# Turning the context rows on VectorE instead of TensorE in the attention stage

## The chip, the cores and the metric

The kernel runs on one core of a Trainium2 chip. The metric is the device time of one execution in microseconds. TensorE multiplies matrices (its results go to PSUM banks), VectorE and ScalarE move and compute between SBUF and PSUM, GpSimd computes on SBUF, and SyncE issues the DMAs. Each engine works through its own queue in order; semaphores connect them.

## What is computed

A layer with cross attention and a feed-forward network, in fp32:

```
x:   [16, 112, 1024]      ctx: [16, 375, 1024]
q = layernorm(x) @ Wq     (32 heads of 32)
k = ctx @ Wk,  v = ctx @ Wv   (8 KV heads of 32, each used by 4 query heads)
x = x + softmax(q k^T / sqrt(32)) v @ Wo
h = silu(y @ w1^T) * (y @ w3^T),  y = layernorm(x)      (inner width 3584)
x = x + h @ w2^T          (weights are w * w_scale per 128x128 block)
```

The products need the 1024 context columns on the partitions, so every context (375 rows of 1024) has to be transposed before K and V can be computed. That transposition is what changes.

## The kernel before

The program has a query stage, the attention stage, an output stage ("mixing") and the feed-forward stage. Every fp32 product is made of three: each operand is split into a high part (rounded to the fp32r type, on ScalarE) and a low part (the rest, `to_lo` on VectorE, line 90), and lines 84 to 86 add high x high, high x low and low x high in PSUM.

The attention stage is written as a pipeline of bodies (`each`). Body b does four things at once for four batches: attention proper for batch b (`attn`), the row maxima of the scores of batch b+1 (`score`), the K and V projections of batch b+2 (`proj`), and the transposition of context b+3 (`trans`). Bodies run from -3 to 15. Body -3 only transposes; bodies -2 and -1 have no attention proper; bodies 0 to 12 do all four; body 13 has no context to transpose; 14 and 15 run out. Each body has 32 steps, and each engine's queue is the list of its work step by step. The tables give the steps:

```
T_STEP = {3: 0, 9: 1, 15: 2, 21: 3, 26: 4, 30: 5}     # step: tile of the context
KV_TILES = 3*[[2,1,1,1,1,2]] + [[2,2,1,1,2],[2,2,2,1,1]]   # K0 K1 V0 V1 V2, from step 1
INV = {25, 27, 28, 31: batch b; 5, 8, 11, 14: batch b-1}    # reciprocals of the sums
```

Per step TensorE scores one head of batch b+1 against all keys (two heads at steps 18 and 24, none at 30 and 31) into one of two banks; VectorE takes the maximum over the keys (L696), and head h is scored only once head h-2 has its maximum. Then come one or two of the eight accumulation steps of a K or V tile, and at steps 6 to 29 a score matmul in the other direction (L907), whose exponential ScalarE takes (L800). At steps 19 and 31 TensorE multiplies the exponentials by V ("PV", L924), at steps 2 and 22 it adds their sums over the partitions (L816). GpSimd first adds the exponentials of three key blocks, per group of 16 heads in two adds of 125x1792: the first (L649) when eight exponentials are there, so after steps 13 and 25, the second (L645) when twelve are; and it scales the result (L656). All these operands of GpSimd are in SBUF. A body ends and begins with the transpose of the maxima at step 0 (L842), whose bank VectorE splits (L688 and L90) for the next steps.

A context tile n before the change is a block of 125 rows by 512 columns (four 128-column pieces). TensorE transposes the four pieces against a unit matrix into one PSUM bank (L861), ScalarE writes the high part `cT_h` from the bank (L774), VectorE the low part `cT_l` (bank minus high), all listed at the tile's step. TensorE begins K of the next batch (step 1 of the next body) when all six tiles have their low part (`t_lo`). The two banks (`pj_bank`) are shared by the transposes, the K and V tiles and the transpose of the maxima; so several waits of TensorE are about banks. Contexts lie row by row in `stash` (two slots of three blocks) and are loaded by three DMAs of 125 rows with 4 KB each, one body ahead.

## Time and profile before

| | |
|---|---|
| median of 3 runs | 2532.99 us (2530.29 to 2537.29) |
| profiled execution | 2538.41 us, span of the profile 2536.6 us |
| TensorE busy, share of the span | 2427.8 us, 96% |
| VectorE | 1698.4 us, 67% |
| ScalarE | 979.2 us, 39% |
| GpSimd | 559.2 us, 22% |
| transposes of the context (L861) | 384 matmuls, first at 191.4, last at 751.7 |
| maxima (L696) | 512, 264.9 us busy |
| attention stage | some 191 to 850 us of the span |

All times below are microseconds from the start of the span, of one profiled execution. A duration in a row is that of one instruction (or the merged run of several, with xcount). Neighbouring instructions of one engine overlap a little, so the price of one more in a full queue is the distance from its start to the next start. Of a matmul the duration contains the way through the array; its price is again the distance between starts. In square brackets behind a row stands how long the engine was idle before it and what ended that.

### The profile page before, as it was taken

How to read it: one execution, taken by the hardware profiler on the slowest of the kernel's cores; microseconds unless marked ns; L12 is line 12 of the kernel's file. 1: busy time of each engine (PE TensorE's matmuls, PEld its weight loads, DVE VectorE, ACT ScalarE, POOL GpSimd, SP SyncE). 2: the span in 40 equal slices, each digit the busy share in tenths (PEclk: the TensorE clock that was granted, in tenths of full speed). 3: DMA queues.
4: the chain of work that ended last, by engine and by line, in shares of the span. 5: the costliest groups of instructions: out<-in, count | busy, mean ns of one | idle time of the engine just before them, and what ended most of it. 6: DMA issues, size and time to landing. Idle time of an engine off the chain costs nothing.

```text
span 2536.6 us, 35412 instructions
## 1 busy us (share of the span) xinstructions
PE 2427.8 (96%) x12682; PEld 2071.4 (82%) x12682; DVE 1698.4 (67%) x2639; ACT 979.2 (39%) x1673; POOL 559.2 (22%) x305
## 2 busy tenths in 40 slices
PE   7998999999999799599999998999999999999999
PEld 6997878878875488489999987988988978888887
DVE  6425777777776344688888888888888874445442
ACT  3212445445444321354444444444433443233231
POOL 1000344454455300001111111322333320000000
PEclk9998999999998799799999999999999999999999
DMA  7535555555545335456555564565776687555652
GB/s 226 173 92 138 140 139 139 144 134 142 143 110 131 95 127 170 119 183 184 159 176 156 158 179 134 158 174 190 208 209 176 172 287 234 172 174 160 183 161 86
DMA packets 369146, 408.04 MB, mean 161 GB/s; under 512 B 125824, under 2 KB 324096, under 8 KB 359152
## 3 DMA queue, kind: packets, MB, share of 16 engines
q1 hardware_dynamic: 369008, 406.22, 56.1%
q8 instruction: 85, 1.39, 0.2%
q14 instruction: 53, 0.43, 0.1%
HBM read 252.99 MB, written 152.70 MB: 160 GB/s over the span
## 4 chain that ended last, share of the span: by engine, by line
PE 44%; DVE 8%; DMA 3%; issue 2%; SPq 1%; ACT 1%; DVEq 0%; ACTq 0%
PE bank L84 15%; PE bank L85 14%; PE bank L86 14%; DMA stash<-weight_scratch 3%; DVE g_WL L90 2%; DVE g_XL L90 1%; DVE g_su L1699 1%; DVE xT L1655 1%; SPq L1431 1%; DVE stash L1667 1%; DVE stash L1666 1%; DVE stash L1669 1%; ACT stash L1548 0%; ACT g_WH L1558 0%; DVE stash L1643 0%
## 5 line engine op out<-in xcount | busy, mean ns | idle before, releaser
L84 PE MATMUL bank<-g_XH,g_WH 128*128 128x448 f32 (+1 forms) x2254 | 848.0, 376 | 51.8 <-DVE g_su L1699 24.2
L85 PE MATMUL bank<-g_XL,g_WH 128*128 128x448 f32 (+1 forms) x2254 | 845.0, 375 | 0.0
L86 PE MATMUL bank<-g_XH,g_WL 128*128 128x448 f32 (+1 forms) x2254 | 844.8, 375 | 0.0
L84 PEld LDWEIGHTS bank<-g_XH,g_WH 128*128 128x128 f32 x2254 | 425.2, 189 | 115.8 <-DVE g_WL L90 52.8
L86 PEld LDWEIGHTS bank<-g_XH,g_WL 128*128 128x128 f32 x2254 | 425.2, 189 | 54.1
L85 PEld LDWEIGHTS bank<-g_XL,g_WH 128*128 128x128 f32 x2254 | 425.4, 189 | 53.5
L1558 ACT ACTIVATE g_WH<-stash 128x512 fp32r<-128x512 f32 x392 | 241.7, 627 | 427.6 <-PE bank L86 247.0
L90 DVE TENSOR_TENSOR g_WL<-stash,g_WH 128x512 fp32r<-128x512 f32 (+1 forms) x417 | 336.0, 809 | 77.4 <-ACT g_WH L1558 49.4
L696 DVE TENSOR_REDUCE a_nm<-bank 112x1 f32<-112x375 f32 x512 | 264.9, 531 | 116.9 <-PE bank L831 113.3
L800 ACT ACTIVATE a_pr<-bank 125x448 f32<-125x448 f32 x384 | 204.8, 545 | 208.2 <-PE bank L907 153.7
L649 POOL TENSOR_TENSOR a_prsum<-a_pr 125x1792 f32<-125x1792 f32 x32 | 129.3, 4039 | 365.3 <-ACT a_pr L800 365.3
L1699 DVE TENSOR_TENSOR g_su<-bank,g_su 128x448 f32<-128x448 f32 x280 | 170.8, 610 | 35.6 <-PE bank L86 35.3
L831 PE MATMUL bank<-a_kst,a_qst 96*112 96x376 f32 x512 | 183.2, 367 | 5.8 <-DVE a_nm L696 2.6
L907 PE MATMUL bank<-a_qst,a_kst 98*125 98x448 f32 x384 | 148.3, 391 | 2.8 <-ACT a_pr L800 2.4
L831 PEld LDWEIGHTS bank<-a_kst,a_qst 96*112 96x112 f32 x512 | 91.7, 179 | 69.7 <-DVE a_nm L696 32.6
L1498 POOL TENSOR_TENSOR g_Sh<-stash 128x448 f32<-128x448 f32 x28 | 32.6, 1165 | 492.5 <-DVE stash L1704 492.5
L645 POOL TENSOR_TENSOR a_prsum<-a_prsum,a_pr 125x1792 f32<-125x1792 f32 x32 | 128.7, 4022 | 1.8
L678 DVE RECIPROCAL a_l<-a_l 128x112 f32<-128x112 f32 x128 | 106.6, 839 | 25.8 <-ACT a_l L754 25.8
L84 PE MATMUL bank<-a_w_h,a_cT_h 128*125 128x256 f32 x384 | 111.8, 291 | 0.0
L86 PE MATMUL bank<-a_w_h,a_cT_l 128*125 128x256 f32 x384 | 107.8, 281 | 0.0
L85 PE MATMUL bank<-a_w_l,a_cT_h 128*125 128x256 f32 x384 | 107.7, 280 | 0.0
L1285 ACT ACTIVATE g_WH<-stash 128x1792 fp32r<-128x1792 f32 x25 | 42.6, 1703 | 156.8 <-PE bank L86 146.3
(132 smaller groups left out, 3592.8 us busy)
## 6 DMA issues: line engine op xcount, KB each, us to landing
stash<-in_L_ffn_w SPq DMA_DIRECT2D x168, 256.0 KB, 5.1
weight_scratch<-stash SPq DMA_DIRECT2D x28, 1024.0 KB, 7.7
stash<-weight_scratch SPq DMA_DIRECT2D x28, 1024.0 KB, 7.4
h_scratch<-g_Sh SPq DMA_DIRECT2D x112, 224.0 KB, 3.9
down_scratch<-xT SPq DMA_DIRECT2D x98, 256.0 KB, 3.1
stash<-in_ctx SPq DMA_DIRECT2D x48, 500.0 KB
stash<-h_scratch SPq DMA_DIRECT2D x25, 896.0 KB, 6.7
a_qst<-q_scratch SPq DMA_DIRECT2D x96, 224.0 KB, 4.7
```

What stands on the lines that cost most here:

```text
L84: pe.matmul(acc, lh, rh, start=first, stop=False, skip_group_check=onto)
L85: pe.matmul(acc, lh, rl, start=False, stop=False, skip_group_check=onto)
L86: return pe.matmul(acc, ll, rh, start=False, stop=last, skip_group_check=onto)
L90: return nc.vector.tensor_tensor(dst, src, hi.bitcast(f32), ALU.subtract)
L645: pool.tensor_tensor(prsum[:], prsum[:], pr[0:CK, :, 2, :], ALU.add).then_inc(all_added, 1)
L649: pool.tensor_tensor(prsum[:], pr[0:CK, :, 0, :], pr[0:CK, :, 1, :], ALU.add).then_inc(two_added, 1)
L696: nc.vector.tensor_reduce(nm[:, 1 - par, h:h + 1], s_bank[h % 2][0:SQ, 0:SK], AX.X, ALU.max, negate=True).then_inc(max_done, 1)
L800: nc.scalar.activation(pr[0:CK, r, c, :], st_bank[u % 2][0:CK, 0:J * SQ], ACT.Exp, scale=SCALE).then_inc(exp_done, 1)
L831: pe.matmul(s_bank[h % 2][0:SQ, 0:SKP], qst[0:96, 1 - par, g, j * SQ:(j + 1) * SQ], kst[0:96, 1 - par, g, :], start=True, stop=True).then_ ...
L907: pe.matmul(st_bank[u % 2][0:CK, 0:J * SQ], kst[0:98, par, g * R + r, c * CK:(c + 1) * CK], qst[0:98, par, g * R + r, :], start=True, stop ...
L1558: nc.scalar.activation(WH[:, i, :, :], w_source(mi, i), ACT.Copy).then_inc(w_hi, 1)
L1699: nc.vector.tensor_tensor(su[:, slot, :], acc[mi % 2][:, 0:TB], su[:, other, :], ALU.add).then_inc(summed, 1)
```

## The change

The context is loaded in another layout, turned on VectorE, and the split reads SBUF. A batch's context is loaded as four column quarters of 256 columns, one on each 32 partitions, with the rows in blocks of 32: eight DMAs with rows of 1 KB. VectorE's transpose turns 32x32 blocks, so a block transpose of 128 partitions by 512 elements (two row blocks) yields tile n: 64 context rows, all 1024 columns, with column q*256 + 32k + j on partition 32q + j of slice k. The K and V weights are loaded with their rows in that same order. The tile is written to a double buffer `ctT` in a part of `stash` that was free.

The transpose stands at the tile's step on VectorE, behind the maxima and the K or V copy of that step. ScalarE makes the high part at the same step, now from `ctT`. VectorE's low part moves one step later (`s - 1 in T_STEP`). TensorE loses the transposes, and its waits for banks are written anew. The Wo load waits for `t_lo` and `t_hi` as well.

```diff
         def load_ctx(sp, n, slot):
-            for c in range(NC):
-                sp.dma_start(ctx_in[:, slot, c, :], ctx[bass.ds(n, 1), c * CK:(c + 1) * CK, :]
-                             .rearrange("b k n -> k (b n)")).then_inc(c_loaded[slot], 16)
+            for q in range(Q4):
+                cols = slice(q * DQ, (q + 1) * DQ)
+                sp.dma_start(ctx_in[q * BL:(q + 1) * BL, slot, 0:CB - 1, :],
+                             ctx[bass.ds(n, 1), 0:CROWS, cols].rearrange("b (c i) n -> i (b c) n", i=BL)
+                             ).then_inc(c_loaded[slot], 16)
+                sp.dma_start(ctx_in[q * BL:q * BL + SK - CROWS, slot, CB - 1, :],
+                             ctx[bass.ds(n, 1), CROWS:SK, cols].rearrange("b k n -> k (b n)")
+                             ).then_inc(c_loaded[slot], 16)
...
                         for n, w in enumerate((wk, wv)):
-                            sp.dma_start(wkv_raw[:, :, n * KV:(n + 1) * KV],
-                                         w.rearrange("(k p) n -> p k n", p=P)
-                                         ).then_inc(wkv_loaded, 16)
+                            for q in range(Q4):
+                                sp.dma_start(wkv_raw[q * BL:(q + 1) * BL, :, n * KV:(n + 1) * KV],
+                                             w[q * DQ:(q + 1) * DQ, :].rearrange(
+                                                 "(k j) n -> j k n", j=BL)).then_inc(wkv_loaded, 16)
...
-                    c, kh = n // 2, n % 2
-                    return cT[:, 1 - par, 4 * kh:4 * kh + 4, c * CK:(c + 1) * CK]
+                    return cT[:, 1 - par, :, 2 * BL * n:min(2 * BL * (n + 1), SK)]
+
+                ctT = stash[:, 2 * NC + 1, :].rearrange("p (e k n) -> p e k n", e=2, k=KT)
+
+                def turned(n):
+                    return ctT[:, n % 2, :, 0:min(2 * BL, SK - 2 * BL * n)]
...
                                 sp.wait_ge(t_done, NT * B)
+                                sp.wait_ge(t_lo, NT * B)
+                                sp.wait_ge(t_hi, NT * B)
                                 sp.wait_ge(v_moved, B)
                                 load_wo(sp)
...
                                 if trans and s in T_STEP:
                                     n = T_STEP[s]
+                                    if n == 0:
+                                        dve.wait_ge(c_loaded[1 - par], 16 * 2 * Q4 * (i + 2 + par))
+                                    wait(dve, t_hi, NT * tb + n - 1)
+                                    wait(dve, t_lo, NT * tb + n - 1)
+                                    nc.vector.transpose(
+                                        ctT[:, n % 2, :, :].rearrange("p b (c j) -> p b c j", j=BL),
+                                        ctx_in[:, 1 - par, 2 * n:2 * n + 2, :].rearrange(
+                                            "p c (b j) -> p b c j", j=BL)).then_inc(t_done, 1)
+                                if trans and s - 1 in T_STEP:
+                                    n = T_STEP[s - 1]
                                     dve.wait_ge(t_hi, NT * tb + n + 1)
-                                    to_lo(cT_part(cT_l, par, n), t_bank(par, n)[:, 0:4 * CK].rearrange(
-                                        "p (k n) -> p k n", k=4), cT_part(cT_h, par, n)
-                                        ).then_inc(t_lo, 1)
+                                    to_lo(cT_part(cT_l, par, n), turned(n), cT_part(cT_h, par, n)
+                                          ).then_inc(t_lo, 1)
...
                                     nc.scalar.activation(cT_part(cT_h, par, n),
-                                                         t_bank(par, n)[:, 0:4 * CK].rearrange(
-                                                             "p (k n) -> p k n", k=4), ACT.Copy
+                                                         turned(n), ACT.Copy
                                                          ).then_inc(t_hi, 1)
...
-                                if trans and s in T_STEP:
...
-                                    if n == NT - 1:
-                                        pe.wait_ge(t_lo, NT * tb + n)
-                                    elif n == 0 and attn:
-                                        pe.wait_ge(nm_lo, b + 1)
-                                    elif proj:
-                                        accumulated(pe, pb, n - 1)
-                                    else:
-                                        wait(pe, t_lo, n - 1)
-                                    for k in range(4):
-                                        kk = 4 * kh + k
-                                        last = pe.transpose(t_bank(par, n)[:, k * CK:(k + 1) * CK],
-                                                            ctx_in[:, 1 - par, c, kk * P:(kk + 1) * P],
-                                                            ident[0:CK, 0:CK])
-                                    last.then_inc(t_done, 1)
...
                                         pe.wait_ge(t_lo, NT * (pb + 1))
+                                        wait(pe, v_out, NC * pb)
                                     elif ks[0] == 0:
-                                        if trans:
-                                            pe.wait_ge(t_lo, NT * tb + m)
-                                        elif m == 1:
-                                            pe.wait_ge(nm_lo, b + 1)
+                                        if m == 1:
+                                            if attn:
+                                                pe.wait_ge(nm_lo, b + 1)
                                         else:
                                             accumulated(pe, pb, m - 2)
```

On VectorE the end of a body, from step 25 to step 31, stands so before. Here `a_nm` are the maxima, `a_l` the sums to be inverted, `a_cT_l` the low part of a context tile, and the COPY moves a V tile:

```order
L696 TENSOR_REDUCE a_nm<-bank 112x1
L678 RECIPROCAL a_l<-a_l 128x112
L696 TENSOR_REDUCE a_nm<-bank 112x1
L90 TENSOR_TENSOR a_cT_l<-bank,a_cT_h 128x4x125
L696 TENSOR_REDUCE a_nm<-bank 112x1
L678 RECIPROCAL a_l<-a_l 128x112
L696 TENSOR_REDUCE a_nm<-bank 112x1
L678 RECIPROCAL a_l<-a_l 128x112
L696 TENSOR_REDUCE a_nm<-bank 112x1
L711 COPY stash<-bank 125x256
L90 TENSOR_TENSOR a_cT_l<-bank,a_cT_h 128x4x125
L678 RECIPROCAL a_l<-a_l 128x112
```

The same stretch after, from the maximum of step 26 on (`stash` is the context and `ctT`):

```order
L705 TENSOR_REDUCE a_nm<-bank 112x1
L729 STREAM_TRANSPOSE stash<-stash 128x512
L705 TENSOR_REDUCE a_nm<-bank 112x1
L90 TENSOR_TENSOR a_cT_l<-stash,a_cT_h 128x8x64
L687 RECIPROCAL a_l<-a_l 128x112
L705 TENSOR_REDUCE a_nm<-bank 112x1
L687 RECIPROCAL a_l<-a_l 128x112
L705 TENSOR_REDUCE a_nm<-bank 112x1
L720 COPY stash<-bank 125x256
L729 STREAM_TRANSPOSE stash<-stash 128x512
L90 TENSOR_TENSOR a_cT_l<-stash,a_cT_h 128x8x55
L687 RECIPROCAL a_l<-a_l 128x112
```

Two transposes have come in, the splits stand a step later, and their first input is `stash` in place of a bank.

On TensorE the end of a body and the start of the next stand so before (the score of the last head, L907, the last transpose group, PV, then the scores of heads 0 and 1 around the transpose of the maxima, and K):

```order
L831 MATMUL bank<-a_kst,a_qst 112x376
L907 MATMUL bank<-a_qst,a_kst 125x448
L861 MATMUL bank<-ident,stash 128x125 x4
L924 MATMUL bank<-a_pr,stash 32x448 x12
L831 MATMUL bank<-a_kst,a_qst 112x376
L842 MATMUL bank<-ident,a_nm 32x112
L831 MATMUL bank<-a_kst,a_qst 112x376
L84 MATMUL bank<-a_cT_h,a_w_h 128x376
```

And after:

```order
L848 MATMUL bank<-a_kst,a_qst 112x376
L902 MATMUL bank<-a_qst,a_kst 125x448
L919 MATMUL bank<-a_pr,stash 32x448 x12
L848 MATMUL bank<-a_kst,a_qst 112x376
L859 MATMUL bank<-ident,a_nm 32x112
L848 MATMUL bank<-a_kst,a_qst 112x376
L84 MATMUL bank<-a_cT_h,a_w_h 128x376
```

The transpose group is gone; the rest keeps its order, and the K product still waits for the last low part.

## Rows read from the trace of the kernel before

**Rows 1.** Busy by stretch: length, busy us by engine (count), clock, DMA share.

```profile
409.93:448.25 38.32, 38.11 (x266) 30.49 (x265) 28.18 (x55) 18.73 (x37) 18.30 (x7) 1.00 0.52 139
...
716.48:754.69 38.21, 38.01 (x266) 30.49 (x265) 28.27 (x54) 18.73 (x37) 18.22 (x7) 1.00 0.41 98
754.69:790.13 35.44, 35.21 (x242) 27.99 (x241) 24.95 (x49) 15.56 (x31) 17.45 (x7) 1.00 0.43 108
```

**Rows 2.** Timeline (start us, duration us), TensorE, a transpose group in body 0.

```profile
260.20 0.34 PE L831 MATMUL bank<-a_kst,a_qst 96*112 96x376 f32 x1
260.37 0.59 PE L861 MATMUL bank<-ident,stash 125*128 125x125 f32 x4
...
260.98 0.33 PE L85 MATMUL bank<-a_cT_l,a_w_h 128*128 128x376 f32 x1
```

**Rows 3.** Timeline, VectorE, bodies 4 and 13.

```profile
421.42 0.68 DVE L90 TENSOR_TENSOR a_cT_l<-bank,a_cT_h 128x500 fp32r<-128x500 f32 x1 [0.24 <-ACT a_cT_h L774]
422.01 0.54 DVE L696 TENSOR_REDUCE a_nm<-bank 112x1 f32<-112x375 f32 x1
...
788.69 0.41 DVE L711 COPY stash<-bank 125x256 f32<-125x256 f32 x1
789.02 0.84 DVE L678 RECIPROCAL a_l<-a_l 128x112 f32<-128x112 f32 x1
```

**Rows 4.** Groups by line and shape (count, busy us, mean ns), VectorE.

```profile
L1643 DVE STREAM_TRANSPOSE stash<-stash 128x512 f32<-128x512 f32 x112 | 75.4, 695 | 7.3 <-ACT stash L1540 7.3
...
L90 DVE TENSOR_TENSOR a_w_l<-stash,a_w_h 128x512 fp32r<-128x512 f32 x8 | 5.3, 683 | 0.0
```

**Rows 5.** Timeline, VectorE, feed-forward stage.

```profile
1214.00 1.65 DVE L1667 TENSOR_TENSOR stash<-stash 128x512 f32<-128x512 f32 x1
```

**Rows 6.** Timeline, GpSimd, the same stretch.

```profile
1213.40 1.70 POOL L1501 TENSOR_TENSOR g_Sh<-g_Sh,stash 128x448 f32<-128x448 f32 x1
```

**Rows 7.** Durations by line or tile, ns min/median/max, first and last start.

```profile
L1667 DVE TENSOR_TENSOR stash<-stash x56: 680/686/1647, 1045.7 to 2031.6; 128x512 f32<-128x512 f32 x56
...
L90 DVE TENSOR_TENSOR a_cT_l<-bank,a_cT_h x96: 667/679/682, 193.2 to 753.3; 128x500 fp32r<-128x500 f32 x96
```

**Rows 8.** Timeline, VectorE, an old context split in body 3.

```profile
408.51 0.67 DVE L90 TENSOR_TENSOR a_cT_l<-bank,a_cT_h 128x500 fp32r<-128x500 f32 x1
```

**Rows 9.** Timeline, GpSimd, bodies 3, 4 and 13.

```profile
408.33 4.03 POOL L645 TENSOR_TENSOR a_prsum<-a_prsum,a_pr 125x1792 f32<-125x1792 f32 x1
...
442.55 4.06 POOL L649 TENSOR_TENSOR a_prsum<-a_pr 125x1792 f32<-125x1792 f32 x1 [6.99 <-ACT a_pr L800]
...
770.03 4.03 POOL L649 TENSOR_TENSOR a_prsum<-a_pr 125x1792 f32<-125x1792 f32 x1 [11.74 <-ACT a_pr L800]
...
785.28 4.04 POOL L649 TENSOR_TENSOR a_prsum<-a_pr 125x1792 f32<-125x1792 f32 x1 [6.11 <-ACT a_pr L800]
```

**Rows 10.** Timeline, ScalarE, body 4.

```profile
442.53 0.59 ACT L774 ACTIVATE a_cT_h<-bank 128x500 fp32r<-128x500 f32 x1
```

**Rows 11.** Timeline, TensorE, body 13.

```profile
754.97 0.34 PE L84 MATMUL bank<-a_cT_h,a_w_h 128*128 128x376 f32 x1
...
772.32 0.66 PE L831 MATMUL bank<-a_kst,a_qst 96*112 96x376 f32 x2
```

**Rows 12.** Busy by stretch, TensorE alone, ahead of body -1.

```profile
225.96:228.93 2.97, 1.00 (x6) 1.00 1.08 212
228.93:232.34 3.41, 3.41 (x14) 0.50 1.09 208
```

**Rows 13.** Timeline, TensorE, start of attention.

```profile
191.42 1.90 PE L861 MATMUL bank<-ident,stash 125*128 125x125 f32 x8 [2.63 <-PEq L238]
...
203.21 0.68 PE L84 MATMUL bank<-a_cT_h,a_w_h 128*128 128x376 f32 x1 [3.19 <-DVE a_w_l L90]
```

**Rows 14.** Timeline, queue of SyncE, body 5.

```profile
452.67 1.20 SPq L143 DMA_DIRECT2D stash<-in_ctx  x3
464.51 0.39 SPq L596 DMA_DIRECT2D k_scratch<-a_k_h  x1
```

More of the change, by code:

```diff
@@ L112, in build_program @@
         stash = top.enter_context(nc.sbuf_tensor("stash", [P, 12, D], f32))
-        ctx_in = stash[0:CK, 0:2 * NC, :].rearrange("p (s c) n -> p s c n", s=2)
+        CB, CROWS = -(-SK // BL), SK // BL * BL
+        ctx_in = stash[:, 0:2 * NC, :].rearrange("p (s c) n -> p s (c n)", s=2).rearrange(
+            "p s (k n) -> p s k n", n=DQ)
         wkv_raw = stash[:, 8:12, :].rearrange("p a (b n) -> p (a b) n", n=2 * KV)
@@ L517, in kv_bank @@
                     return pj_bank[(m + par) % 2]
-                def t_bank(par, n):
-                    return pj_bank[(n + (n < NT - 1) + par) % 2]
                 def nm_bank(par):
@@ L741, in _ @@
                     def _(act):
-                        act.wait_ge(wkv_loaded, 32)
+                        act.wait_ge(wkv_loaded, 32 * Q4)
                         def copy_out(b, g):
@@ L843, in body @@
                                                  ident[0:SQ, 0:SQ]).then_inc(nmT_done, 1)
-                                if trans and s in T_STEP:
-                                    n = T_STEP[s]
-                                    c, kh = n // 2, n % 2
-                                    if n == 0:
-                                        pe.wait_ge(c_loaded[1 - par], 16 * NC * (i + 2 + par))
-                                    if n == NT - 1:
-                                        pe.wait_ge(t_lo, NT * tb + n)
-                                    elif n == 0 and attn:
-                                        pe.wait_ge(nm_lo, b + 1)
-                                    elif proj:
-                                        accumulated(pe, pb, n - 1)
-                                    else:
-                                        wait(pe, t_lo, n - 1)
-                                    for k in range(4):
-                                        kk = 4 * kh + k
-                                        last = pe.transpose(t_bank(par, n)[:, k * CK:(k + 1) * CK],
-                                                            ctx_in[:, 1 - par, c, kk * P:(kk + 1) * P],
-                                                            ident[0:CK, 0:CK])
-                                    last.then_inc(t_done, 1)
                                 if proj and s in KV_AT:
```

## The prediction

> **What bounds the kernel now.** I first read the busy table by stretch. The change touches the attention stage only, so I cut that stage into bodies, one per query batch, at the matmul of L842 that opens each. In a steady body TensorE is busy 38.1 of 38.3 us and VectorE 28.2; body 13, the first that transposes no context, takes 35.44 us with TensorE again busy throughout, against 38.21 for the body before it [rows 1]. So TensorE sets the pace, and the transposes cost it some 2.8 us a body. The timeline of TensorE says the same from below: matmuls follow each other at 0.17 us, but from the start of a group of four transposes (260.37) to the second K product behind it (260.98) 0.61 us pass; without the group that product would stand 0.17 behind 260.37 [rows 2]. That is 0.44 us a group, six groups a body, 2.6 us. Since VectorE is busy in 28 of 38 us, has to follow TensorE head by head (the maximum of head h-2 must be taken before head h is scored) and receives the moved work, its order and its waits have to be read next, and then the GpSimd rows, because the new operands lie elsewhere.
>
> **What goes.** Sixteen contexts times six groups leave TensorE. Thirteen bodies (0 to 12) do attention and transposes together. If nothing else came last, each would fall to about body 13's 35.4 us: 13 x 2.8 = 36 us.
>
> **What comes on VectorE, without waits.** Start to start in a full queue, a maximum takes 0.46 us, a reciprocal 0.76, a split of a context tile 0.59 and the copy of a V tile 0.33: each row's duration less the 0.08 by which the next one overlaps it [rows 3]. A block transpose of 128x512 took 695 ns, a split of 128x512 with both inputs in SBUF 683 ns [rows 4]; less the same overlap that is 0.61 and 0.60. The new splits cover 512 elements instead of 500 and read SBUF instead of PSUM: equal within 0.01. So the change adds 6 x 0.61 = 3.7 us a body. Adding up the queue of a body now (32 maxima 14.7, 8 reciprocals 6.1, 6 splits 3.5, 2 K splits 0.9, 3 copies 1.0, the V move 0.5, and 0.4 for the maxima's own split) gives 27.1 us; after, 30.8. That would fit into 35.4 us, were it spread evenly. It isn't: steps 24 to 31 hold 7 maxima, 4 reciprocals, 2 copies, 2 transposes and 2 splits.
>
> **What comes as a wait: the port.** The old split read a PSUM bank and the high half. The new one reads two SBUF tensors. In the feed-forward stage VectorE has such adds (L1667) while GpSimd adds in SBUF too: one took 1.65 us and ended at 1215.65, some 0.55 us behind the end of a GpSimd add (1213.40 + 1.70 = 1215.10) [rows 5, 6]. The 56 instructions of that line take 0.69 us in the median and up to 1.65; the 96 old splits of the context, with their PSUM input, never leave 0.67 to 0.68 [rows 7]. One of these ran at 408.51, inside the GpSimd sum that took 4.03 us from 408.33 [rows 8, 9]. So a new split that comes upon a GpSimd sum waits for its end, and everything queued behind it on VectorE waits too. The Trainium skill states this as a rule (SBUF — State Buffer, section "SBUF: two separate sides"): VectorE and GpSimd share a port pair under an exclusive lock, which a VectorE instruction with two SBUF inputs takes against a GpSimd one that reads SBUF, and the loser is blocked for the whole instruction. By that rule the wait is certain for this operand pair; by the rows alone it is carried over from another stage. Without it the sum would be the second case below.
>
> GpSimd's sums take 4.0 us, four a body, and they start where the splits do. The first sum of a head group starts when eight exponentials are there (steps 13 and 25 on ACT; 770.03 and 785.28 in body 13) [rows 9]. Split 2 comes at step 16 and split 4 at step 27; ACT makes the high half of tile 4 right after the exponential that releases the sum (442.53 on ACT [rows 10], the sum 442.55), so split 4 comes behind the start of that sum, and by less than 4 us. Both meet a sum in every body.
>
> **The path through a new body**, counted from the first K product (754.97 in body 13 [rows 11]).
> The first sum starts at 770.03 in body 13, 15.1 us in. Transpose 1 and split 1 fall into steps 9 and 10, beside the V move, a K split and two reciprocals; steps 7 to 12 then hold 6.4 us for VectorE and 5.9 for TensorE (five steps of 0.9 and one of 1.4). With hand-overs I take 0.7 us of delay. The sum ends at 15.1 + 0.7 + 4.0 = 19.8, split 2 at 20.4, the maximum of head 17 at 20.9, and head 19 can be scored. In body 13 that was at 772.55 (the second of the pair at 772.32), 17.6 in. Delay: 3.3 us.
> From there to the next sum nothing new is long (split 3 finds the port free, as the matmuls of step 19 let VectorE catch up). That sum starts at 785.28 in body 13, 30.3 in; now 33.6.
> Then in a row: the sum 4.0, split 4 0.6, reciprocal, maximum, reciprocal, maximum, copy, transpose 5 (0.76 + 0.46 + 0.76 + 0.46 + 0.33 + 0.61 = 3.4), ACT's high half 0.59 with two hand-overs of 0.08, split 5 0.68 and a hand-over: 0.7. The next K product waits for split 5 (its tile completes the context), at 33.6 + 4.0 + 0.6 + 3.4 + 0.75 + 0.74 = 43.1 us. The second sum of the group starts behind split 4 and ends as split 5 comes, so it adds nothing.
> A body goes from 38.3 to 43.1 us: +4.8, times 13 is **+62 us**.
>
> **The clock.** Between the end of the PV matmuls of step 31 and the K product TensorE then has some 3.5 us with a transpose and two scores. A stretch of that kind is in the trace: from 225.96 to 228.93 TensorE was busy 1.00 of 2.97 us, and in the next 3.41 us the granted clock was 0.50, the lower level of 1.2 GHz [rows 12]. At half clock 3.41 us lose 1.7 us of TensorE work. Bounds per body: nothing (it never falls) and two such stretches, 3.4. Part of it lies where TensorE would wait for VectorE anyway. I take 0.9 us, 13 bodies, **+12**.
>
> **The start.** The first context is turned with TensorE idle either way, and the first K product stood at 203.21 [rows 13], 11.8 us behind the first transpose. Now a tile costs transpose, ACT copy, split and weight split in a row (0.75 + 0.66 + 0.60 + 0.60 = 2.6 us), six tiles and two more weight splits 16.8 us: +5. The two bodies without attention give back 1.3 (behind it a DMA is awaited) and 1.5, and less of the first K products runs at the half clock, 0.8. Net +1.4. Bounds: +5 and -1.
>
> **At nothing.** The context load becomes eight DMAs of 1 KB rows instead of three of 4 KB. SP issued the three in 1.20 us at 452.67 and then had until 464.51 before the K stores [rows 14]; eight at 0.4 are 3.2 us. Each tile is needed a whole body later. If that cover failed, transpose 0 would wait at step 3 and with it the maxima. The wkv loads in eight pieces lie beside the query stage. The added waits on t_lo and t_hi before the Wo load have long passed in body 14. ACT reads SBUF instead of PSUM: 0.03 us a tile.
>
> **Sum** against the profiled execution, 2538.4 us: 2538.4 + 62 + 12 + 1.4 = 2614. The median of the runs is 5.4 below that execution: 2609.
>
> **Rivals.**
> 1. *The queue alone* (14%). The port isn't contended in attention. VectorE's new work then still delays the path: by 0.7 us at steps 9 to 12, by about 1.4 at steps 15 to 18 (transpose 2 and split 2, 1.2, and a hand-over), and at the end. In body 13 the last copy is through at 789.02 [rows 3]; behind it now come transpose 4, split 4, transpose 5, ACT and split 5 (0.61 + 0.60 + 0.61 + 0.75 + 0.74 = 3.3), so K starts at 792.3 and not 35.44 behind the last one, at 790.4: 1.9. Body: 35.4 + 2.1 + 1.9 = 39.4 against 38.3. 13 x 1.1 + 1.4 = 16 us more, time 2549. For it: no row of attention shows this operand pair beside GpSimd. Against: rows 5 to 7.
> 2. *TensorE still last, faster* (6%). VectorE's backlog is absorbed by its idle time, which is mostly behind the PV matmuls. It decides if the splits reach the port before the sums. Then 13 x 2.8 = 36 less, 3 less early, 5 more at the start: 2499. Against: the order of ACT ties split 4 behind the sum's start, and the step sums above.
> 3. *The clock in every body at its bound, or late contexts* (5%): above 2642 by 13 x 3.4 instead of 13 x 0.9.
> A result within 0.3% would need port waits of a fifth of those above: 3%.
>
> **How the numbers follow.** My forecast (72%) is 2609, its own range 2585 to 2642. The range to hold 8 in 10 takes in the first rival: 2543 to 2642. Faster or slower by more than 0.3%, some 8 us, is about what a measurement of this kernel can tell from no change. Faster 0.07, same 0.04, slower 0.89.
>
> **What would show it.** Right: splits of context tiles of about 2 and 3 us or longer at steps 16 and 27, ending 0.6 us behind a GpSimd sum; bodies of about 43 us; TensorE waiting for split 5 ahead of the first K product, a VectorE busy share that includes the waits; half-clock stretches in bodies 0 to 12. Wrong: splits of 0.68 throughout (rival 1), bodies of 35 to 36 us (rival 2), VectorE idle at step 3 for a context. The forecast is most exposed in the two delays by the port, which are differences of start times, and in the clock.

## The result

The changed kernel takes 2658.7 us (median, 2651.9 to 2664.0) against 2532.6 us (2530.3 to 2537.3) for the kernel before: a ratio of 1.049, with a 95% interval of 1.046 to 1.053. It is slower, as forecast, but by 126 us and not by 76, and it lies outside the range I gave. The profiled execution has a span of 2661.5 us (2536.6 before) and a mean granted clock of 0.947 (0.977 before).

### The profile page after: what moved, and what is told of

It is laid out like the page before. It is cut to its first block, busy times and chain, and to the rows that moved or that the text cites. A ratio compares the mean times of both kernels' runs of the same rounds, so it can differ in the third digit from the quotient of the medians.

```text
span 2661.5 us, 34971 instructions
## 1 busy us (share of the span) xinstructions
PE 2463.4 (93%) x12298; PEld 2072.4 (78%) x12298; DVE 1798.4 (68%) x2735; ACT 974.1 (37%) x1673; POOL 567.1 (21%) x305
## 4 chain that ended last, share of the span: by engine, by line
PE 43%; DVE 7%; DMA 3%; issue 2%; SPq 1%; ACT 1%; DVEq 0%; ACTq 0%
PE bank L84 14%; PE bank L86 14%; PE bank L85 14%; DMA stash<-weight_scratch 3%; DVE g_WL L90 2%; DVE g_XL L90 1%; SPq L1426 1%; DVE g_su L1694 1%; DVE xT L1650 1%; DVE stash L1661 1%; DVE stash L1662 1%; DVE stash L1664 1%; ACT stash L1543 0%; ACT g_WH L1553 0%; DVE stash L1638 0%
## 5 line engine op out<-in xcount | busy, mean ns | idle before, releaser
L86 PEld LDWEIGHTS bank<-g_XH,g_WL 128*128 128x128 f32 x2254 | 425.4, 189 | 54.3
L817 ACT ACTIVATE a_pr<-bank 125x448 f32<-125x448 f32 x384 | 198.0, 541 | 215.6 <-PE bank L902 111.6
L848 PE MATMUL bank<-a_kst,a_qst 96*112 96x376 f32 x512 | 194.6, 386 | 36.4 <-DVE a_nm L705 31.1
L848 PEld LDWEIGHTS bank<-a_kst,a_qst 96*112 96x112 f32 x512 | 97.8, 191 | 108.2 <-DVE a_nm L705 63.3
L902 PE MATMUL bank<-a_qst,a_kst 98*125 98x448 f32 x384 | 156.2, 409 | 21.9 <-ACT a_pr L817 21.4
L792 ACT ACTIVATE a_cT_h<-stash 128x512 fp32r<-128x512 f32 x96 | 59.6, 621 | 245.8 <-DVE stash L729 245.8
L90 DVE TENSOR_TENSOR a_cT_l<-stash,a_cT_h 128x512 fp32r<-128x512 f32 x96 | 112.6, 1173 | 36.6 <-ACT a_cT_h L792 36.5
L84 PE MATMUL bank<-a_cT_h,a_w_h 128*128 128x376 f32 x256 | 97.3, 380 | 39.0 <-DVE a_w_l L90 19.6
```

What stands on the lines that cost most here:

```text
L84: pe.matmul(acc, lh, rh, start=first, stop=False, skip_group_check=onto)
L86: return pe.matmul(acc, ll, rh, start=False, stop=last, skip_group_check=onto)
L90: return nc.vector.tensor_tensor(dst, src, hi.bitcast(f32), ALU.subtract)
L817: nc.scalar.activation(pr[0:CK, r, c, :], st_bank[u % 2][0:CK, 0:J * SQ], ACT.Exp, scale=SCALE).then_inc(exp_done, 1)
L848: pe.matmul(s_bank[h % 2][0:SQ, 0:SKP], qst[0:96, 1 - par, g, j * SQ:(j + 1) * SQ], kst[0:96, 1 - par, g, :], start=True, stop=True).then_ ...
L902: pe.matmul(st_bank[u % 2][0:CK, 0:J * SQ], kst[0:98, par, g * R + r, c * CK:(c + 1) * CK], qst[0:98, par, g * R + r, :], start=True, stop ...
```

## The profile after the change

The busy table and the clock row of the page, shares of the span and then tenths in 40 slices:

```profile
PE 2463.4 (93%) x12298; PEld 2072.4 (78%) x12298; DVE 1798.4 (68%) x2735; ACT 974.1 (37%) x1673; POOL 567.1 (21%) x305
...
PEclk9998888888888979989999999999999999999999
```

The clock digits of slices 4 to 13, most of the attention stage, are all 8. Cut at the matmul of L859 (L842 before), the bodies 0 to 12 take 45.0, 47.3, then 47.7 to 47.9 us each, and 46.2 at the end; before, they took 38.2 on average. Busy time by stretch, body 4 first, then body 13, which transposes nothing (columns: length; busy time of PE, PEld, DVE, ACT and POOL with their instructions; granted clock; DMA share; GB/s). They answer to [rows 1]:

```profile
452.30:500.07 47.77, 41.93 (x241) 31.29 (x241) 35.08 (x61) 18.27 (x36) 19.00 (x7) 0.86 0.51 111
...
880.82:918.98 38.16, 36.80 (x242) 29.07 (x243) 26.64 (x51) 16.16 (x32) 16.05 (x7) 0.96 0.37 90
```

TensorE now idles 5.8 us in a body. It has about as many matmuls in it as body 13 of the kernel before (35.2 us busy) and is busy for 41.9 us, since part of the body runs at half clock. VectorE's 35.1 us contain waits that the profile counts as work. Its timeline in body 4, at the steps that the prediction named (start, duration, engine, line, operation, out<-in, shapes, and the idle time ahead of it):

```profile
472.21 0.84 DVE L687 RECIPROCAL a_l<-a_l 128x112 f32<-128x112 f32 x1
472.97 0.48 DVE L705 TENSOR_REDUCE a_nm<-bank 112x1 f32<-112x375 f32 x1
473.38 0.69 DVE L729 STREAM_TRANSPOSE stash<-stash 128x512 f32<-128x512 f32 x1
474.00 0.51 DVE L705 TENSOR_REDUCE a_nm<-bank 112x1 f32<-112x375 f32 x1
474.77 1.85 DVE L90 TENSOR_TENSOR a_cT_l<-stash,a_cT_h 128x512 fp32r<-128x512 f32 x1 [0.27 <-ACT a_cT_h L792]
...
494.24 3.13 DVE L90 TENSOR_TENSOR a_cT_l<-stash,a_cT_h 128x512 fp32r<-128x512 f32 x1 [0.27 <-ACT a_cT_h L792]
497.30 0.84 DVE L687 RECIPROCAL a_l<-a_l 128x112 f32<-128x112 f32 x1
...
499.62 0.40 DVE L720 COPY stash<-bank 125x256 f32<-125x256 f32 x1
499.94 0.69 DVE L729 STREAM_TRANSPOSE stash<-stash 128x512 f32<-128x512 f32 x1
501.27 0.62 DVE L90 TENSOR_TENSOR a_cT_l<-stash,a_cT_h 128x440 fp32r<-128x440 f32 x1 [0.64 <-ACT a_cT_h L792]
```

And GpSimd's timeline in the same body:

```profile
472.05 4.02 POOL L658 TENSOR_TENSOR a_prsum<-a_pr 125x1792 f32<-125x1792 f32 x1 [15.95 <-ACT a_pr L817]
476.03 1.58 POOL L665 TENSOR_TENSOR a_o<-a_o,a_l 128x448 f32<-128x448 f32 x1
...
492.78 4.04 POOL L658 TENSOR_TENSOR a_prsum<-a_pr 125x1792 f32<-125x1792 f32 x1 [11.21 <-ACT a_pr L817]
496.90 4.31 POOL L654 TENSOR_TENSOR a_prsum<-a_prsum,a_pr 125x1792 f32<-125x1792 f32 x1
```

Read the two together. The first sum ends at 472.05 + 4.02 = 476.07, split 2 at 474.77 + 1.85 = 476.62. The second group's first sum ends at 496.82, split 4 at 497.37. Both splits end 0.55 us behind a sum, the figure of [rows 5, 6], and a split that meets no sum takes 0.69. Over all 96 splits the tile's row has 616 ns, a median of 693 and a longest of 3130, where [rows 7] had 667 to 682. The reciprocal of 472.21 and the block transpose of 473.38 lie wholly inside a sum and take their usual 0.84 and 0.69. Of VectorE's instructions in these two sums only the one that reads two SBUF tensors waits.

What TensorE waited for from 404.55 to 834.67, nine bodies (total, times, longest):

```profile
PE bank L848 <- DVE a_nm L705: 17.0, 18, 1.3
PE bank L902 <- ACT a_pr L817: 13.4, 27, 0.9
PE bank L84 <- DVE a_cT_l L90: 12.9, 9, 1.4
PE bank L859 <- DVE stash L720: 9.5, 9, 1.1
```

That is 5.9 us a body. Of these, 4.4 stand behind the splits: head 19 behind split 2, and at the end of the body a score, the maxima's transpose and the first K product (0.60, 1.05 and 1.43).

```profile
475.22 0.47 PE L902 MATMUL bank<-a_qst,a_kst 98*125 98x448 f32 x1 [0.92 <-ACT a_pr L817]
477.13 0.65 PE L848 MATMUL bank<-a_kst,a_qst 96*112 96x376 f32 x1 [1.26 <-DVE a_nm L705]
...
501.94 0.68 PE L84 MATMUL bank<-a_cT_h,a_w_h 128*128 128x376 f32 x1 [1.43 <-DVE a_cT_l L90]
```

The other 1.5 us are waits for ScalarE's exponentials (L817). The kernel before had no such waits; run 1 shows where they come from. The granted clock, by stretch:

```profile
452.80:459.60 6.80, 5.43 (x19) 3.54 (x20) 3.28 (x8) 1.09 (x2) 1.77 (x2) 0.50 0.50 104
459.60:476.70 17.10, 15.01 (x85) 13.35 (x84) 15.84 (x28) 9.18 (x18) 4.65 (x2) 1.00 0.58 131
476.70:483.50 6.80, 6.37 (x28) 4.34 (x32) 2.26 (x5) 0.30 (x1) 4.87 (x2) 0.50 1.04 216
483.50:500.60 17.10, 15.13 (x114) 10.06 (x106) 13.73 (x21) 7.71 (x16) 7.74 (x2) 1.00 0.25 53
```

The first low stretch begins as TensorE waits for the first K product of the body, the second as it waits for head 19. Each steady body has both, 13.6 of its 47.8 us at 1.2 GHz; before, bodies 0 to 12 had none.

## The experiments

Each run was timed beside the kernel before. My theory was that a body's 9.5 extra us are three things: VectorE's longer queue, the splits' waits for GpSimd's sums, and a clock that falls because of these waits. The first rival was that the queue alone does it.

**1. The split without the SBUF operand.** It reads unused columns of a PSUM bank, so the turned context does not enter the low half. Waits that keep the bank's users apart are left out of the diff.

```
+                def flat(n):                          # zeros, one row repeated over k
+                    w = min(2 * BL, SK - 2 * BL * n)
+                    src = o_bank if n == 3 else l_bank
+                    return src[:, 448:448 + w].rearrange("p (o n) -> p o n", o=1).broadcast_to([P, KT, w])
...
-                                    to_lo(cT_part(cT_l, par, n), turned(n), cT_part(cT_h, par, n)
+                                    to_lo(cT_part(cT_l, par, n), flat(n), cT_part(cT_h, par, n)
```

> The changed kernel, but the split of a context tile takes its first operand from a few unused columns of a PSUM bank (zeros, repeated) and not from the SBUF tile that was turned; everything else, the block transposes too, stays. The low halves are wrong by that. Theory (the port is what waits, and the half clock follows from those waits): all splits 0.6 to 0.75 us, none longer in bodies 0 to 12; body 39 to 41 us; low-clock stretches rare; time 2540 to 2580. Rival (the extra work in VectorE's queue is what costs, wherever the operands lie): splits may be short, but the body stays above 45 us and the time above 2630.

Measured: 2560.4 us, ratio 1.010 (1.008 to 1.012). All 96 splits took 616 to 693 ns. A steady body took 39.8 us at full clock, no low stretch between 270 and 823 us (columns as above):

```profile
462.89:502.75 39.86, 36.77 (x242) 27.93 (x241) 31.45 (x61) 18.16 (x36) 18.29 (x7) 1.00 0.60 134
```

98 of the 126 us, the low clock's share with them, hang on where the split reads from; the instructions and their order are as in the changed kernel. What is left, 39.8 against 38.2 us a body, is the price of the queue, which rival 1 had put at 39.4. It isn't VectorE's queue alone. TensorE waits 3.0 us a body: 0.9 for split 5, 0.6 for maxima, and 1.5 for exponentials, as in the changed kernel. ScalarE and TensorE, at the place of split 2:

```profile
482.70 0.63 ACT L807 ACTIVATE a_cT_h<-stash 128x512 fp32r<-128x512 f32 x1 [1.27 <-DVE stash L739]
483.24 1.62 ACT L832 ACTIVATE a_pr<-bank 125x448 f32<-125x448 f32 x3
...
483.81 0.46 PE L917 MATMUL bank<-a_qst,a_kst 98*125 98x448 f32 x1 [0.93 <-ACT a_pr L832]
```

ScalarE's high half waits for VectorE's block transpose, the exponentials stand behind it in ScalarE's queue, and TensorE waits for one of them. VectorE also waits 0.8 us a body ahead of split 0 for one of this run's own bank waits, so the queue of the changed kernel may cost a little less than 1.6 us.

**2. The same operand in the kernel before.** TensorE keeps its transposes; nothing is added in the bodies.

```
-    to_lo(cT_part(cT_l, par, n), t_bank(par, n)[:, 0:4 * CK]..., cT_part(cT_h, par, n))
+    to_lo(cT_part(cT_l, par, n), stash[:, 7, 0:4 * CK]..., cT_part(cT_h, par, n))    # zeros in SBUF
```

> The kernel before, TensorE's transposes and all, with one edit: the split of a context tile reads its first operand from an SBUF slot of the same size (zeros) and not from the PSUM bank. The low halves are wrong by that; no instruction is added. Theory (port): the splits at steps 15 and 26 or one of them take 2 to 4 us, they end 0.6 us behind a GpSimd sum, TensorE waits there and falls to the half clock; 60 to 120 us more than the kernel before, time 2590 to 2650. Rival (operands don't matter): splits 0.68, time within 8 us of 2533.

Measured: 2650.3 us, ratio 1.047 (1.044 to 1.049), just beyond the upper edge. VectorE's splits and GpSimd's sums of body 5 of this kernel:

```profile
505.23 0.68 DVE L90 TENSOR_TENSOR a_cT_l<-stash,a_cT_h 128x500 fp32r<-128x500 f32 x1 [0.24 <-ACT a_cT_h L778]
511.55 3.23 DVE L90 TENSOR_TENSOR a_cT_l<-stash,a_cT_h 128x500 fp32r<-128x500 f32 x1
...
531.07 3.94 DVE L90 TENSOR_TENSOR a_cT_l<-stash,a_cT_h 128x500 fp32r<-128x500 f32 x1 [0.45 <-ACT a_cT_h L778]
538.03 3.40 DVE L90 TENSOR_TENSOR a_cT_l<-stash,a_cT_h 128x500 fp32r<-128x500 f32 x1
```

```profile
510.22 4.02 POOL L650 TENSOR_TENSOR a_prsum<-a_pr 125x1792 f32<-125x1792 f32 x1 [14.50 <-ACT a_pr L804]
...
530.47 4.00 POOL L650 TENSOR_TENSOR a_prsum<-a_pr 125x1792 f32<-125x1792 f32 x1 [10.73 <-ACT a_pr L804]
536.90 3.99 POOL L646 TENSOR_TENSOR a_prsum<-a_prsum,a_pr 125x1792 f32<-125x1792 f32 x1 [2.43 <-ACT a_pr L804]
```

Three splits a body wait, each until 0.54 us behind the end of a sum (514.24 and 514.78; 534.47 and 535.01; 540.89 and 541.43). One operand, with no other change, costs the kernel before 119 us (2650.3 against 2531.7).

A steady body takes 47.7 us, as in the changed kernel, with less of the low clock and longer waits. Bodies 2 to 6 have one low stretch of 3.4 us and bodies 8 to 12 have two. Body 5, then body 10:

```profile
491.49:539.19 47.70, 40.30 (x267) 31.17 (x266) 36.64 (x55) 18.69 (x37) 18.66 (x7) 0.96 0.42 111
729.90:777.60 47.70, 41.96 (x266) 32.33 (x266) 36.73 (x55) 18.91 (x37) 18.67 (x7) 0.93 0.43 112
```

The second stretch makes TensorE busy for 1.7 us more, and yet the body does not get longer: in this kernel it is hidden behind the waits.

**3. The changed kernel kept at the full clock.** Idle matmuls, whose results nobody uses, stand where TensorE waited. Added waits for a bank are left out of the diff.

```
+    def fill(to, count):
+        for _ in range(count):
+            pe.matmul(to[:, 0:448], w_h[:, 0, 0:P], w_h[:, 1, 0:448], start=True, stop=True)
...
+    fill(st_bank[0], 3)      # behind the PV matmuls of step 31
+    fill(st_bank[0], 5)      # step 0, ahead of the transpose of the maxima
+    fill(st_bank[0], 7)      # step 1, ahead of the first K product
+    fill(o_bank, 4)          # step 17, ahead of the score matmul
+    fill(o_bank, 6)          # step 18, ahead of head 19
```

> The changed kernel with idle matmuls (128x448, 0.19 us each, results unused) put into TensorE's queue where it waited: 3 behind the PV matmuls of step 31, 5 ahead of the matmul of L859, 7 ahead of the first K product, 4 ahead of the score matmul of step 17 and 6 ahead of head 19. Theory (the half clock is a cost of its own, some 4.7 us a body): granted clock 1.0 in bodies 0 to 12, VectorE's waits as they were, body 43 to 44.5, time 2600 to 2625. Rival (the half clock lies beside waits that bound the body anyway): the body stays at 47 to 48 and the time at 2650 or above, since matmuls were added.

Measured: 2602.7 us, ratio 1.028 (1.026 to 1.030): 56 us faster for 25 more matmuls a body. No low stretch in bodies 0 to 12; the splits wait as before (1.87 and 3.12 us in the body shown).

```profile
478.39:521.42 43.03, 41.92 (x266) 32.19 (x266) 35.08 (x61) 18.17 (x36) 19.13 (x7) 1.00 0.56 124
```

So the half clock costs 47.8 - 43.1 = 4.7 us a body. This run is also the test of the forecast's path, without the clock. Counted from its first K product at 480.26:

| | forecast | with idle matmuls | changed kernel, body 4 |
|---|---|---|---|
| first sum starts | 15.8 | 16.0 (496.29) | 17.9 (472.05) |
| split 2 ends | 20.4 | 20.6 (500.89) | 22.5 (476.62) |
| second group's sum starts | 33.6 | 33.9 (514.13) | 38.6 (492.78) |
| next K product | 43.1 | 43.1 | 47.8 |

**4. The sums in pieces.** Each GpSimd sum as four adds (R is 4), here the second of a group; the first is cut in the same way.

```
-                                pool.tensor_tensor(prsum[:], prsum[:], pr[0:CK, :, 2, :], ALU.add
-                                                   ).then_inc(all_added, 1)
+                                for r in range(0, R, R // 4):
+                                    rr = slice(r, r + R // 4)
+                                    done = pool.tensor_tensor(prsum[:, rr, :], prsum[:, rr, :],
+                                                              pr[0:CK, rr, 2, :], ALU.add)
+                                done.then_inc(all_added, 1)
...
```

> The changed kernel with each GpSimd sum (125x1792) written as four of 125x448, the semaphore on the last. Theory (a split waits for the GpSimd instruction that it met, not for the sum): splits of at most 0.7 + 1.1 = 1.8 us, body 41 to 43.5, time 2565 to 2610. Rival (VectorE waits until GpSimd runs out of work): splits up to 3 us as before, time 2650 or above.

Measured: 2581.8 us, ratio 1.020 (1.017 to 1.022), body 40.9 from body 3 on, with no low stretch. Bodies 1 and 2 have two low stretches of 3.4 us each and take 43.8. The three splits that meet a sum take 0.98, 1.18 and 1.35 us:

```profile
493.18 1.18 DVE L90 TENSOR_TENSOR a_cT_l<-stash,a_cT_h 128x512 fp32r<-128x512 f32 x1 [0.27 <-ACT a_cT_h L798]
...
509.08 1.35 DVE L90 TENSOR_TENSOR a_cT_l<-stash,a_cT_h 128x512 fp32r<-128x512 f32 x1 [0.27 <-ACT a_cT_h L798]
```

The split waits for the instruction that it met, not for GpSimd to run out of work. The Trainium skill (SBUF — State Buffer, section "SBUF: two separate sides") states that the lock on the shared port pair holds for one whole instruction. This trace agrees, with 3.13 us cut to 1.35 when only the length of GpSimd's instructions changed. The price is a longer sum, 4.9 against 4.0 us.

**5. Idle matmuls at the end of the body alone.** Those of run 3 at steps 17 and 18 are left out, the waits for the bank there stay.

> The changed kernel with the idle matmuls at the end of the body alone (3 behind the PV matmuls of step 31, 5 ahead of the matmul of L859, 7 ahead of the first K product) and none at steps 17 and 18. Theory (each of the two low stretches is set off by the wait just before it): the stretch behind the first K product goes, the one behind head 19 stays; body 45 to 46 us, time 2625 to 2645. Rival (the two low stretches have one cause, the long wait at the end): both go, body 43, time 2605; or neither does, 2655.

Measured: 2619.8 us, ratio 1.034 (1.033 to 1.036), body 44.5. The stretch at the end is gone and the other one stays, so the waits at the end are not needed for the one at head 19. The time is 5 us below what I had given, because the one that stays is half as long as in the changed kernel, which neither theory had said:

```profile
508.40:511.80 3.40, 3.39 (x14) 3.32 (x15) 1.69 (x4) 0.00 (x0) 3.40 (x2) 0.50 1.02 225
```

One stretch of 3.4 us costs 44.5 - 43.1 = 1.4 us a body. Run 4 says the same: its two stretches cost 43.8 - 40.9 = 2.9 us.

**6. Another table.** The changed kernel with other steps, no work or operand changed.

```
-    T_STEP = {3: 0, 9: 1, 15: 2, 21: 3, 26: 4, 30: 5}
+    T_STEP = {1: 0, 5: 1, 11: 2, 17: 3, 21: 4, 23: 5}
```

> The changed kernel with another table of steps alone: tiles 0 to 5 are turned at steps 1, 5, 11, 17, 21 and 23 and no longer at 3, 9, 15, 21, 26 and 30, each split one step later as before. All work and all operands stay. Splits 2 and 4 then come ahead of, or between, the GpSimd sums, split 5 no longer stands between the last copy and the first K product. Theory (what costs is where the splits meet the sums and the end of the body): body 36.3 to 38.3 us, hardly a low-clock stretch, time 2505 to 2540. Rival (3.7 us more of VectorE work can't be placed anywhere, some other wait takes its place): body over 40 us, time over 2570.

Measured: 2518.8 us, ratio 0.9935 (0.991 to 0.996), body 36.5 and no low stretch from 235 to 774 us. Two splits a body still wait (1.68 and 1.58 us), and TensorE doesn't wait for any; what it waits for is GpSimd's sum, 1.0 us a body:

```profile
441.12:477.62 36.50, 35.45 (x242) 28.06 (x241) 32.92 (x60) 18.41 (x36) 18.74 (x7) 1.00 0.65 146
```

**7. Tables for each part of a tile.**

```
-    T_STEP = {3: 0, 9: 1, 15: 2, 21: 3, 26: 4, 30: 5}
+    T_STEP = {0: 0, 1: 1, 4: 2, 18: 3, 19: 4, 23: 5}
+    H_STEP = {1: 0, 4: 1, 11: 2, 19: 3, 20: 4, 24: 5}     # high half, ACT
+    L_STEP = {2: 0, 5: 1, 12: 2, 20: 3, 21: 4, 24: 5}     # split, VectorE
```

> As the last, with tables of their own for the three parts of a tile: turned at steps 0, 1, 4, 18, 19 and 23, high halves on ACT at 1, 4, 11, 19, 20 and 24, splits at 2, 5, 12, 20, 21 and 24, so that VectorE doesn't wait for ACT in between and the context is ready eight steps before the end. Theory: body 35.7 to 37.5 us (TensorE last again, 35.4 in the body without transposes), time 2495 to 2525, faster than both kernels. Rival (splits 3 and 4 now meet the second sum of the first head group, and the wait is paid again): body 39 or more, time over 2550.

Measured: 2506.1 us, ratio 0.989 (0.988 to 0.991), body 36.3. The same kernel once more, beside run 9:

> The kernel with tables of its own once more, for the comparison on one chip: body 36.3 us, ratio to the kernel before 0.989 as there.

Measured: 2512.4 us, ratio 0.991 (0.989 to 0.993). TensorE had one wait left, over ten bodies (328 to 691 us):

```profile
PE bank L835 <- POOL a_prsum L656: 9.7, 10, 1.1
```

**8 and 9. The last wait, read wrongly and then rightly.** The row above doesn't say at which of the two steps the adding up of the sums waits. I took it for the first group's.

```
-    SUMS = {2: (1, 1), 22: (0, 0)}
+    SUMS = {2: (1, 1), 23: (0, 0)}      # run 8
+    SUMS = {3: (1, 1), 22: (0, 0)}      # run 9
```

> As the run with tables of its own for the three parts of a tile (2506 us), and TensorE's adding up of the first head group's sums stands at step 23 and no longer at 22. In the run before TensorE waited 1.0 us there in every body for the second GpSimd sum, since everything ahead of it had become faster. Theory (that wait is all that stands between 36.3 and the 35.4 us of a body that TensorE alone sets): body 35.4 to 35.7, time 2491 to 2500. Rival (the wait moves on, to the reciprocals and the end of the body): body 36.2 to 37, time 2504 to 2515.

Measured: 2513.5 us, ratio 0.991 (0.989 to 0.993), body 36.7, and the same 9.7 us of waiting. The theory fell. TensorE's timeline of the kernel with step 22 shows the place, 3.1 us behind the first K product of a body:

```profile
404.45 0.96 PE L835 MATMUL bank<-a_prsum,a_ones 125*32 125x448 f32 x8 [1.01 <-POOL a_prsum L656]
```

> Again the kernel with tables of its own (2506 us), SUMS at 22 as there, but the adding up of the second head group's sums at step 3 and no longer at 2. The run with step 23 had rested on a wrong reading: the wait of 1.0 us stands at step 2 (404.45, for the GpSimd sum that began at 400.31), not at 22. Theory (that wait is what stands between 36.3 us and a body that TensorE alone sets): body 35.4 to 35.6, time 2492 to 2500. Rival (the wait moves on to the copy and the reciprocals of steps 4 and 5, or to GpSimd's next sum): body 36.2 or more, time 2504 or more.

Measured: 2495.8 us, ratio 0.9865 (0.984 to 0.989), body 35.6 to 35.8, no wait of TensorE left:

```profile
434.22:469.84 35.62, 35.52 (x243) 27.95 (x241) 31.95 (x60) 18.52 (x36) 19.07 (x7) 1.00 0.69 150
```

This is the best version: 1.35% faster than the kernel before, 6% faster than the changed one. TensorE is busy 35.5 of 35.6 us, as in the body without transposes of [rows 1]. The bodies explain 8 of the 16.6 us between this run and the kernel of run 7 timed beside it (463.2 against 471.3 us for bodies 0 to 12). What lies behind body 13 holds none of the moved work; it took 1738.0 us in the profiled execution here, 1746.5 there, and 1737 to 1747 over all runs.

## Why the prediction was right or wrong

**The bound and what goes: right.** TensorE set the pace and the transposes cost it 2.8 us a body. Run 9 collects that: its bodies 0 to 12 take 463.2 us and those of the kernel before 497.1, 2.6 us less each.

**VectorE's queue: right in kind.** A block transpose took 0.69 to 0.71 us and a split 0.69, as priced [rows 4]. With the port out of the way (run 1) a body takes 39.8 us, 1.6 more than before, where rival 1 said 1.1. I had priced VectorE's queue and not what it does to ScalarE's: the exponentials that wait behind a high half cost TensorE 1.5 us of waits a body in run 1, as in the changed kernel.

**The port: right, shown in both directions.** Taking the SBUF operand out of the changed kernel removes the waits; putting it into the kernel before makes them. They stood at splits 2 and 4, as named.

**The path: right to 0.3 us at each point,** as the table under run 3 shows. At full clock the steady body takes 43.1 us as forecast, and bodies 0 to 12 of run 3 take 60 us more than those of the kernel before, where I had 62. The port's share of that is 43.1 - 39.8 = 3.2 us (43.07 and 39.81 before rounding), the queue's 1.6. Most of the port's share is split 4: at the start of the second group's sum, run 1 is only 0.7 us ahead of run 3 (33.1 and 33.9 us in), where my two cases were 1.2 apart.

**The clock: the step that failed.** I took one low stretch a body, as long as the one of [rows 12], half of it hidden: 0.9 us, with 3.4 as the bound for two. There are two stretches a body of 6.8 us each, and they cost 4.7 us a body, above my bound. Three things went wrong. I looked only at the wait between the PV matmuls and the first K product, although my own path had head 19 come 3.3 us late; that is where the second stretch begins. I took the length of the one stretch in the trace (3.41 us) for the length of every one. And I counted on waits for VectorE to hide half of it. Run 5 has one stretch of 3.4 us in a body, and it costs 1.4 us, not 0.9: little of the 1.7 us that TensorE loses in it is hidden. In the changed kernel the two stretches lose (5.43 + 6.37) / 2 = 5.9 us of TensorE's work and cost 4.7. In run 2 a stretch costs nothing. The difference fits the path, which in the changed kernel runs through TensorE's own work up to each of GpSimd's sums and in run 2 through the longer waits; no run took this apart further. Why a stretch is 6.8 us long here and 3.4 in run 5 is open. Over the 13 bodies the change costs 119 us; run 3, without the low clock, 60; so the clock costs 59 where I had 12. That term is the miss. The start below adds 5.5 us to what I had and body 13 adds 2.7; behind them the changed kernel's profiled execution was 4 us shorter than that of the kernel before.

**The start: 6.9 us and not 1.4.** The chain of a tile was as priced. VectorE's timeline of the changed kernel, where one transpose follows the other at 2.6 us:

```profile
193.22 0.71 DVE L729 STREAM_TRANSPOSE stash<-stash 128x512 f32<-128x512 f32 x1 [1.40 <-PEq L245]
...
195.90 0.70 DVE L729 STREAM_TRANSPOSE stash<-stash 128x512 f32<-128x512 f32 x1
...
210.03 0.70 DVE L729 STREAM_TRANSPOSE stash<-stash 128x512 f32<-128x512 f32 x1
```

From the first to the seventh are 16.8 us, the number I had. But the first one began at 193.22, where TensorE's began at 191.42 [rows 13], because the query stage ended 1.8 us later in this execution; no run says whether the change does that. The first K product came at 210.16, 6.9 later, and at 208.2 to 210.1 in runs 1 and 3 to 6, which start in the same way. The 3.6 us that I expected the bodies without full work to give back didn't come: from that product to the first transpose of maxima are 54.3 us, 54.4 before. TensorE's timelines of the kernel before and of the changed one show why:

```profile
227.93 0.60 PE L831 MATMUL bank<-a_kst,a_qst 96*112 96x376 f32 x2 [1.98 <-DMA a_qst<-q_scratch]
...
233.90 0.97 PE L848 MATMUL bank<-a_kst,a_qst 96*112 96x376 f32 x2 [5.01 <-DMA a_qst<-q_scratch]
```

A load of the K and Q stacks is awaited there, and it stands behind the K store in the queue: both were issued 5 to 6 us later than before. TensorE reached this wait 18.7 us behind the first K product, where it had taken 22.7, and waited 3.0 us longer. Behind the wait it lost another 0.9 us, with a low stretch of 6.8 us (231.0 to 237.8) where the kernel before has 3.4. I had named the awaited DMA myself, and then credited a saving ahead of it. In run 7, where tile 1 is turned ahead of split 0, the first K product stands at 204.8 (206.2 in the same kernel once more).

**At nothing: right.** The context's eight DMAs were issued from 457.50 to 461 (3.3 us from the first to the last, 3.2 forecast), and no block transpose waited for a context. Body 13, which has no transposes left, took 2.7 us more than before, as it begins with a late K product and at the low clock; that I had not counted.

**The rivals.** "TensorE still last" is what the changed operation can do with another table (runs 6 to 9), not what this order does. Its condition, splits that reach the port ahead of the sums, was right in the main; it is stricter than needed, since in run 9 one split a body still waits (1.51 us at 457.93) and TensorE waits for nothing. The rival that I gave 5%, the clock at its bound, is nearest to what happened, and even its bound was too low.

## What to carry to other kernels

Before work moves to VectorE, look up where its operands lie and what GpSimd does at that step: a subtraction of two SBUF tensors that takes 0.69 us alone took 3.1 beside a 4 us sum, and the order was worth 163 us (2658.7 against 2495.8 for the same instructions at other steps). Work that comes into one engine's queue can hold up another's: here the exponentials, which stand on ScalarE behind a high half that waits for VectorE's transpose (1.5 us of TensorE's waits a body). Where an edit makes TensorE wait in the middle of dense work, price each place where it waits with a half-clock stretch of its own. How much of the loss counts depends on what the path runs through: 1.4 of 1.7 us where it ran through TensorE's work (run 5), nothing where it ran through longer waits (run 2). Idle matmuls at those places tell in one run what the clock costs, and another table of steps tells whether an edit is bad or only badly placed.

## What the hardware showed

- GpSimd waits as well. Its scaling of 128x448 took 1.58 us behind split 2 and 1.14 otherwise, and its second sum 4.31 us where split 4 got the port first, 4.0 otherwise (run 1 has 1.15 and 4.02 at these places).
- In steady bodies of the changed kernel the clock alternated between 17.1 us at the upper level and 6.8 at the lower, although TensorE was busy 15.0 of each 17.1 us. No single wait of TensorE was longer than 1.43 us.
- Ending one of the two low stretches made the other one shorter, 3.4 for 6.8 us (run 5). Why is open.
